# A Mamba and ternary FFN block on one core: x turned by DVE and DMA from the third block on, the first FFN up product in the second unit, fewer state steps at both ends

## The reference, cut to what matters

```
xn = layernorm(x)                                # x: 2 x 2048 tokens, 512 features
xz = xn @ in_proj_w.T;  x_branch, z = split(xz)  # 1024 features each
x_branch = silu(conv1d(x_branch, 4 taps) + conv_b)
X, dt, B, C = split(x_branch @ x_proj_w.T)
dt = softplus(dt @ dt_proj_w.T + dt_proj_b)
Y = ssd(X * dt, -exp(A_log) * dt, B, C) + X * D   # chunked scan with a carried state
attn = (Y * silu(z)) @ out_proj_w.T
hidden = sigmoid(xn @ q(w1).T) * (xn @ q(w2).T)   # 1408 wide
out = x + attn + hidden @ q(w3).T
q(w) = clip(round(w / (mean(abs(w)) + 1e-8)), -1, 1)
```

## Time and profile before

| what | value |
|---|---|
| median of 3 runs | 1642.5 us (1642.33 to 1643.32) |
| profiled execution | 1641.94 us, its span 1639.8 us |
| granted clock, whole span | 0.99 |
| PE, DVE, ACT, POOL busy | 1574.9, 1201.3, 890.4, 531.8 us |
| length of one block from block 1 on | 195.9 us |

### The profile page before, as it was taken

One profiled execution on the slowest core, in us unless ns is written; L12 is line 12 of the kernel. 1 busy time (PEld: TensorE's weight loads), 2 busy tenths in 40 slices (PEclk: granted clock), 3 DMA queues, 4 the chain that ended last, 5 costly groups with the idle time before them and its releaser, 6 DMA issues.

```text
span 1639.8 us, 25533 instructions
## 1 busy us (share of the span) xinstructions
PE 1574.9 (96%) x9206; PEld 757.0 (46%) x9206; DVE 1201.3 (73%) x1868; ACT 890.4 (54%) x1848; POOL 531.8 (32%) x502
## 2 busy tenths in 40 slices
PE   6788899999999999999999999999999999999999
PEld 3334444544444444444445444444444444444444
DVE  7877876698566985689746996569955698567972
ACT  6686526565356644466355663646535564456641
POOL 4246673243033421234121431314403243133320
PEclk9899899999999999999999999999999999999999
DMA  7154430142102330133201332023310233002420
GB/s 262 63 175 138 148 108 14 60 106 72 35 27 68 99 93 1 40 84 91 72 7 47 88 86 59 8 59 91 83 46 27 62 94 94 10 27 73 103 58 26
DMA packets 175613, 119.08 MB, mean 73 GB/s; under 512 B 125280, under 2 KB 127072, under 8 KB 175488
## 3 DMA queue, kind: packets, MB, share of 16 engines
q1 hardware_dynamic: 175488, 117.46, 25.3%
HBM read 94.09 MB, written 23.33 MB: 72 GB/s over the span
## 4 chain that ended last, share of the span: by engine, by line
PE 86%; issue 3%; DVE 2%; POOL 2%; ACT 2%; DMA 1%; DVEq 0%; POOLq 0%; SPq 0%; ACTq 0%
PE bank L564 18%; PE bank L674 17%; PE bank L692 9%; PE bank L474 9%; PE bank L647 9%; PE bank L458 9%; PE bank L484 4%; PE bank L596 3%; PE bank L608 2%; PE bank L581 2%; POOL less L1615 1%; PE bank L441 1%; ACT edc L923 1%; PE bank L631 1%; PE bank L496 0%
## 5 line engine op out<-in xcount | busy, mean ns | idle before, releaser
L564 PE MATMUL bank<-wx_hi,arena 128*128 128x512 f16 x1024 | 320.0, 383 | 0.0
L674 PE MATMUL bank<-xt_hi,q 128*128 128x512 f16 x704 | 267.8, 380 | 0.1
L674 PE MATMUL bank<-xt_lo,q 128*128 128x512 f16 x704 | 267.7, 380 | 0.0
L1583 POOL TENSOR_TENSOR xst<-xdt,dst 128x512 f32<-128x512 f32 x64 | 66.8, 1043 | 487.2 <-DVE xdt L1241 487.2
L564 PE MATMUL bank<-wx_lo,arena 128*128 128x512 f16 x512 | 196.1, 383 | 0.0
L692 PE MATMUL bank<-q,arena 128*128 128x512 fp8e4 x704 | 163.7, 381 | 0.0
L923 ACT ACTIVATE edc<-csl,csv 128x128 f32<-128x128 f32 x512 | 155.6, 387 | 0.8 <-DMA csl<-sums 0.8
L564 PEld LDWEIGHTS bank<-wx_hi,arena 128*128 128x128 f16 x1024 | 101.1, 99 | 115.1 <-issue 4.3
L1287 DVE TENSOR_TENSOR edc<-edc,gt 128x512 f32<-128x512 f32 x128 | 129.1, 1048 | 31.4 <-ACT edc L928 31.3
L1604 POOL TENSOR_TENSOR yac<-yac,xs 128x512 f32<-128x512 f32 x64 | 95.4, 1491 | 152.4 <-DVE yac L1308 152.4
L962 ACT CAST arena<-full 128x512 f16<-128x512 f32 x88 | 54.5, 619 | 148.0 <-DVE full L1354 148.0
(11 more groups left out here) (219 smaller groups left out, 3539.5 us busy)
## 6 DMA issues: line engine op xcount, KB each, us to landing
csl<-sums SPq DMA_DIRECT2D x128, 256.0 KB, 3.7
y_squares<-xs SPq DMA_DIRECT2D x56, 256.0 KB, 2.0
yac<-y_squares SPq DMA_DIRECT2D x168, 64.0 KB, 2.5
res<-x SPq DMA_DIRECT2D x32, 256.0 KB, 3.0
out<-res SPq DMA_DIRECT2D x32, 256.0 KB, 2.0
raw<-w_ffn SPq DMA_DIRECT2D x25, 256.0 KB, 2.9
full<-w_ffn SPq DMA_DIRECT2D x17, 256.0 KB, 4.2
yac<-x SPq DMA_DIRECT2D x16, 256.0 KB, 3.7
```

The source lines that it names most:

```text
L564: i = pe.matmul(banks[0][:], act[:, k, c * P:(c + 1) * P], wt[:, k, hf * half:(hf + 1) * half], start=(n == 1), stop=(n == 3 * ki))
L674: i = pe.matmul(up_bank(m, j)[:], q12[:, j, m, k, :], part[:, k, :], start=(n == 1), stop=(n == 2 * kd))
L1583: pool.tensor_tensor(by_head(xst[:], hd), by_head(xdt[:], hd), heads_over(sml["dst"][:, c, :], hf * hph, hph, hd), ALU.mult).then_inc(S["x ...
```

## The change

Six things.

1. From block 2 on x is not turned by PE. DVE transposes the normalised chunks in 32x32 squares (`squares_of_x`, four more transposes a block), SP writes them to DRAM and reads them back in four DMAs of 256 KB each, runs of 32 floats (`turn_x`, issued behind the up products). ACT and DVE make `xt_hi` and `xt_lo` from SBUF. `turn(b + 1)` stays for block 1 alone. The first `x_branch` product moves to (0, 8), the last to (1, 10) (`FOLLOWING_LATER`).
2. The next block's x is loaded ahead of `load_res(b, 3)`, and the statistics are done two chunks at a time beside up products 2 and 3, the root beside 4, the normalising and the squares beside 5 and 6.
3. In blocks 1 to 7 PE does `ffn_up(b, 0)` at the end of unit 1, ahead of `project_z(b, 3)`, and no longer at the end of unit 6. ACT and DVE take its result where they did.
4. In block 0, units 0 to 3 have no state (it is zero): no `off_mm`, no yoff, no `sd`, no `y_skip`, and the state is written, not added to. The six memsets of it go.
5. In block 7, units 4 to 7 don't make a state that nobody reads: no `xe`, no `xst`, no `st_mm`, no `state`, no `st_hi` and `st_lo`. In its `ffn_down` chunks 2 and 3 come one behind the other.
6. The weight preparation has another order: scales come one or more steps later behind their sums, the last cuts beside the FFN are 1 and 3 steps in place of 2 and 2, and the last ternary pieces of DVE come behind `turned(1)` and `hid_lo(0, 10)`.

```diff
+FEWER = {"off_mm": 4, "yoff": 4, "sd": 4, "y_skip": 4}
+BESIDE_FFN = [2, 2, 2, 2, 2, 2, 2, 1, 3]
+FOLLOWING_LATER = {(0, 8): 0, (0, 10): 1, (1, 0): 2, (1, 2): 3, (1, 4): 4, (1, 6): 5, (1, 8): 6, (1, 10): 7}
...
-    prep = list(kinds("O M O M O M O M  O M O M O M O M  M M M S M M M B  T M T M T M M M  T M T M T M T S "
-                      "M T M B T M M T  M T M T M M M M  M T S T B T " + "T T " * beside_ffn))
+    prep = list(kinds("O M O M O M O M  O M O M O M O M  M M M S M M M M  M B M T M T M T  M T M T M T S M "
+                      "M T M T B T M T  M T M T M M M M  S T T T T B " + "T " * sum(BESIDE_FFN)))
...
+        def x_squares(j):
+            return x_dram.rearrange("c (i a) (k j b) -> j a k (c i) b", a=SQ, b=SQ, j=P // SQ)[j]
...
+            def turn_x(b):
+                for c in range(chunks):
+                    sp.wait_ge(S["x_blocks"], at(b - 2, "x_blocks", c))
...
+                    sp.dma_start(x_dram[c], xsq[c]).then_inc(D["x_out"], DMA)
+                sp.wait_ge(D["x_out"], (b - 1) * chunks * DMA)
+                for j in range(P // SQ):
+                    sp.dma_start(xall[j * SQ:(j + 1) * SQ].rearrange("a k (n b) -> a k n b", b=SQ),
+                                 x_squares(j)).then_inc(D["x_sq_in"], DMA)
...
+                    if b and b < nb - 1 and m == 0:
+                        for c in range(chunks):
+                            load_x(b + 1, c)
+                    if b and b < nb - 1 and m == 7:
+                        turn_x(b + 1)
...
-                    update(b, u)
+                    if goes_on(b, u):
+                        update(b, u)
...
+                    if b and u == 1:
+
+                        ffn_up(b, 0)
                     if u + 2 < len(units):
                         project_z(b, u + 2)
-                    elif b and u == 6:
-                        ffn_up(b, 0)
...
-                if b < nb - 1:
+                if b == 0:
                     turn(b + 1)
...
+                for together in ((0,), (1,), (2, 3)) if b < nb - 1 else ((0,), (1,), (2,), (3,)):
...
+            def squares_of_x(b, c):
+                dve.wait_ge(S["xn"], at(b, "xn", c))
+
+                dve.wait_ge(S["diag_mm"], at(b - 1, "diag_mm", 12 + c))
+                dve.transpose(xsq[c], xin[c]).then_inc(S["x_blocks"], 1)
...
+                    elif b and b < nb - 1:
+                        if m in (2, 3):
+                            statistics(b + 1, 2 * m - 4)
+                            statistics(b + 1, 2 * m - 3)
+                        elif m == 4:
+                            root(b + 1)
+                        elif m in (5, 6):
+                            for c in (2 * m - 10, 2 * m - 9):
+                                normalise(b + 1, c)
+                                squares_of_x(b + 1, c)
+                if b < nb - 1:
+                    turned(b + 1)
+                hid_lo(b, kf - 1)
                 if b == 0:
                     for kind, n in last:
                         prep_second(kind, n)
-                if b < nb - 1:
-                    turned(b + 1)
-                hid_lo(b, kf - 1)
```

More of the change, by code:

```diff
@@ L122, in mamba_ffn_block @@
               *(f"early{n}" for n in range(6)),
-              *(f"beside{n}" for n in range(4)), "sums_out", "sums_in0", "sums_in1",
-             "y_out0", "y_out1", "y_in0", "y_in1")}
+              "beside0", "beside1", "sums_out", "sums_in0", "sums_in1",
+             "y_out0", "y_out1", "y_in0", "y_in1", "x_out", "x_sq_in")}
         def sb(name, shape, dt=F32):
@@ L188, in mamba_ffn_block @@
         xsp = [sb(f"xst_{p}", [P, half], F16) for p in ("hi", "lo")]
-        yac = [sb(f"yac{n}", [P, half]) for n in range(2)]
-        gate = [sb(f"gate{n}", [P, half]) for n in range(2)]
-        xin = [*yac, *gate]
+        xall = sb("xin", [P, chunks, dm])
+        xin = [xall[:, c] for c in range(chunks)]
+        yac, gate = xin[0:2], xin[2:4]
         edc = [sb(f"edc{n}", [P, hpg * P]) for n in range(2)]
@@ L267, in landing @@
                 s, landed = slot(4, n - n_early)
-                return ffn_ring[s], D[f"beside{s}"], landed
+                if s < 2:
+                    before = len(range(2 + s, len(loaded), 6))
+                    return ffn_ring[s], D[f"early{2 + s}"], before * DMA + landed
+                return ffn_ring[s], D[f"beside{s - 2}"], landed
             s, landed = slot(6, loaded.index((kind, n)))
@@ L446, in x_branch @@
                 bk = banks[4 + m % 4]
+                if b > 1 and m < 4:
+                    name, n = (("y_added", 7), ("yoff", 7), ("state", 7), ("attn", 3))[m]
+                    pe.wait_ge(S[name], at(b - 1, name, n))
                 if m == 0 and b:
@@ L790, in turned @@
                 for k in ks:
-                    act.wait_ge(S["x_turned"], at(b, "x_turned", k))
+                    if b < 2:
+                        act.wait_ge(S["x_turned"], at(b, "x_turned", k))
+                    elif k == 0:
+                        act.wait_ge(D["x_sq_in"], (b - 1) * (P // SQ) * DMA)
                     if b and k == 0:
                         act.wait_ge(S["up_mm"], at(b - 1, "up_mm", 21))
-                    act.copy(xt[0][:, k, :], banks[4 + k][:]).then_inc(S["xt_hi"], 1)
+                    act.copy(xt[0][:, k, :], banks[4 + k][:] if b < 2 else xin[k]).then_inc(S["xt_hi"], 1)
             def x_branch(b, m):
@@ L808, in x_branch @@
                                ACT.Copy, scale=1.0 / (XN_SCALE * W_SCALE)).then_inc(S["raw"], 1)
+                if b > 1 and m == 4:
+                    act.wait_ge(D["x_out"], (b - 1) * chunks * DMA)
                 if b:
@@ L883, in project_x @@
                     act.wait_ge(D[f"y_out{u % 2}"], rounds(b, u) * DMA)
+                elif u >= 2 and not has_state(b, u - 2):
+                    act.wait_ge(S["y_added"], at(b, "y_added", u - 2))
                 elif u >= 2:
@@ L1071, in scalar_program @@
                         project_z(b, u + 2)
[L1072 removed]
+                    if goes_on(b, u):
+                        split_state(b, u)
                 for m in range(kf):
@@ L1618, in gpsimd_program @@
             pool.memset(mhalf[:], -0.5).then_inc(S["cleared"], 1)
-            for b in range(batches):
-                pool.memset(state[b][:], 0.0).then_inc(S["cleared"], 1)
-                for part in state_parts[b]:
-                    pool.memset(part[:], 0.0).then_inc(S["cleared"], 1)
             pool.memset(hal[:], 0.0).then_inc(S["cleared"], 1)
```

135 lines of the change are left out of this document (87 added, 48 removed).

## The result

The changed kernel took **1617.15 us** (median of 4, 1615.01 to 1617.57), the kernel before, on the same chip, 1642.83 us. The ratio is 0.984, 95% interval 0.983 to 0.986: faster by 25.7 us. The forecast was 1620.7 us, 21.8 us faster, so it was short by 3.9 us of gain.

What follows compares the result with a forecast made beforehand. PE was taken as the bound (96% busy, seven of eight blocks packed at 195.9 us). Gains 9.8 + 1.2 + 2.6 + 2.0 + 6 + 0.2 = 21.8 us from 1641.94 gave 1620.1, with 0.6 for the median 1620.7; range 1610 to 1634.

Steps and rivals of the forecast that it cites:

- x turned by DVE and DMA: Turn of x for six blocks: sixteen PE transposes go, net 1.64 us a block, 9.8 us in all.
- The DMA term: Reads of x's squares: 7.8 us to issue four, 1.9 to land; taken as zero cost, at most 12 us.
- the slack of 0.7 us: End of the up products: x's squares land at 832.9, on time by 0.7 us for ACT's xt_hi.
- Rival A: x's squares land late, up to 2.0 us in each of six blocks: 1622 to 1633 us; chance 0.22.
- The first up product: Moved to unit 1: covers PE's scan waits, 1.97 us a block; DVE's residual sum leaves 0.2, 1.2 us in blocks 1 to 6.
- Block 7: Last block: 2.6 us from 12 state matmuls gone, and 2.0 us from the moved up product kept whole.
- the 0.2 at the end: End of the last block: DVE starts on chunk 3, alone last, 0.2 us earlier.
- Block 0: Missing state products and reordered weight preparation: 12.8 us touched, half taken as gain, 6 us; bounds -2 to 12.8.
- B: DVE doesn't hold PE at attn(2), the 1.97 us stays whole, 10.6 us more: 1610 us; chance 0.08.
- C: Turn's gain lost behind it, as dt waits for DVE's s_lo and out_ready(2); 9.8 not gained: 1630 us; chance 0.09.
- D: Slower: x's reads don't overlap, 40 us, ending 30 late: 1800 us; decides from 3.7 us late; chance 0.06.
- E: No change: block 0 gives nothing, C holds, the DVE bound costs 4 us: about 1641 us; chance 0.05.

Runs made afterwards that it cites:

- e1: Changed kernel with the first up product of blocks 1 to 7 back at the end of unit 6: 1622.27 us, ratio 0.988.
- e3: Changed kernel with x turned by PE again in all blocks and loaded as before: 1630.09 us, ratio 0.992.
- e2: Changed kernel with DVE's second residual sum of blocks 1 to 7 moved ahead of y's low half: 1615.89 us, ratio 0.983.
- e7: Changed kernel with normalisation and squares of x in blocks 1 to 6 one up product later on DVE: 1660.32 us (one run).
- e6: Changed kernel with block 7 making its state again for the second half of its units: 1621.37 us, ratio 0.987.
- e5: Changed kernel with block 0 carrying its zero state through the first four units again, memsets back: 1616.44 us, ratio 0.984.
- e4: Changed kernel with the whole old order of block 0's weight preparation: 1621.63 us, ratio 0.987.
- e10: Changed kernel with the second half of the old preparation order (cuts 2 everywhere, last ternary pieces ahead of turned(1)): 1618.54 us, ratio 0.985.
- e9: e2 with, in addition, all four normalisations and squares of x at up product 5 on DVE: 1611.17 us, ratio 0.981.

## Why the prediction was right, and where it was off

**x turned by DVE and DMA: right in size.** Forecast 1.64 us a block; e1 gives 1.67, the undisturbed blocks of e3 1.6 to 1.9. The DMA term was also near: the four reads landed 10.1 us after the first issue (619.18 to 629.28), forecast 7.8 + 1.9 = 9.7, though by another split (5.8 to issue, and more to land) and for another reason: the forecast let each issue cost 1.94 us by its 2048 runs, and the first of each four takes 0.57. That the sum came near is luck. The write took 2.04 us (617.14 to 619.18), as taken from the earlier trace rows. But the slack of 0.7 us wasn't there: the last square ended 11.9 us ahead of the last hidden product (617.14, 629.06) where 12.3 was forecast, and the landing took 0.4 more. The recorded sign for this, "ACT's xt_hi released by PE, not by a DMA", failed in four blocks of six; in the changed kernel:

```profile
629.28 2.18 ACT L851 CAST xt_hi<-xin 128x512 f16<-128x512 f32 x4 [1.42 <-DMA xin<-x_squares]
```

PE paid 0.5 us in all for it, because it was 0.9 us later anyway for the residual sum. Rival A was thus right on the mechanism and wrong on the price in this kernel; e2 shows the price once the other cap is gone, and e7 how steep it is behind that.

**The first up product: the term that was mis-sized.** Forecast 0.2 us a block, measured 0.7. The form was right: no wait at unit 2's scan, and a new one at `project_out` 6 that the residual sum ends, in blocks 1 to 6 and not in block 7. It is 0.91 us, not 1.7 (1.56 in block 1, behind a late read-back):

```profile
786.34 0.63 ACT L1015 ACTIVATE yt_hi<-xs 128x512 f16<-128x512 f32 x1 [4.86 <-DMA xs<-y_squares]
...
787.43 0.67 DVE L1421 SCALAR_TENSOR_TENSOR yt_lo<-xs,yt_hi 128x512 f16<-128x512 f32 x1
788.82 0.68 DVE L1433 SCALAR_TENSOR_TENSOR res<-bank,res 128x512 f32<-128x512 f32 x1
...
789.56 0.39 PE L696 MATMUL bank<-wo_hi,yt_hi 128*128 128x512 f16 x1 [0.91 <-DVE res L1433]
```

The failing step is the reading of 799.14 as the place of the sum in "DVE without a gap". In the kernel before, that block had a gap: DVE's low half of y waited for a late read-back of Y. The same places there, first in the block that was read, then in block 6:

```profile
797.27 0.63 ACT L953 ACTIVATE yt_hi<-xs 128x512 f16<-128x512 f32 x1 [6.00 <-DMA xs<-y_squares]
797.93 0.69 DVE L1331 SCALAR_TENSOR_TENSOR yt_lo<-xs,yt_hi 128x512 f16<-128x512 f32 x1 [0.61 <-ACT yt_hi L953]
799.14 0.68 DVE L1343 SCALAR_TENSOR_TENSOR res<-bank,res 128x512 f32<-128x512 f32 x1
...
1384.01 0.63 ACT L953 ACTIVATE yt_hi<-xs 128x512 f16<-128x512 f32 x1 [5.04 <-DMA xs<-y_squares]
1384.94 0.67 DVE L1331 SCALAR_TENSOR_TENSOR yt_lo<-xs,yt_hi 128x512 f16<-128x512 f32 x1
1386.32 0.68 DVE L1343 SCALAR_TENSOR_TENSOR res<-bank,res 128x512 f32<-128x512 f32 x1
```

Against the first x_branch of its block (641.54 and 1229.24) the sum stands at 157.60 and at 157.08. So 0.52 us of the 1.7 were a late DMA. It was no single bad block: in blocks 1 to 7 the sum stands at 157.74, 157.32, 157.60, 157.33, 158.17, 157.08 and 157.08, late in five of seven. What the forecast didn't see is that this lateness mostly goes in the changed kernel (one block of six, the one of 1.56 us), and nothing shows why it goes. DVE's lateness from the moved product was 0.46 and not 0.65 (the sum at 788.82 is 115.79 behind the block's first B product at 673.03; the undisturbed 157.08 is 115.33 behind it). 1.7 - 0.52 - 0.19 = 0.99, against 0.91 to 0.92 measured. In six blocks (0.7 - 0.2) x 6 = 3.0 us. In the two profiles the span fell by 24.6 us, 2.8 more than the forecast's 21.8, and the six blocks by 12.4, where the forecast's terms (9.8 + 1.2, less the 1.3 of the moved down matmuls) gave 9.7: the miss lies here. The medians' 3.9 differ from this by what the runs scatter.

**Block 7: right.** 2.6 + 2.0 were forecast. e1 gives 2.0 for the up product, e6 3.6 for the state, because with it the wait of 1.0 us comes back: the forecast had put that into the other term. The last stretch fell by 6.1 us; the forecast's share there was 6.1: 2.6, 2.0, the 0.2 at the end, and 1.3 for three pairs of down matmuls that now stand ahead of the first x_branch. No run tried the 0.2 by itself; from the start of the last matmul to the end of the span it is 3.9 us before (1635.91) and 3.6 after (1611.59).

**Block 0: the right number for half a reason.** 6 was forecast, taken as half of 12.8, and the two profiles differ by 6.03. But 2.6 of the 12.8 us were PE's products with the missing state, and e5 shows that part, with DVE's 2.4 that stood beside the sum, at 0.5, nothing that could be told; the order of the preparation is worth 5 to 6 by e4. Half of 12.8 was a choice and no working, so that it came out is luck. (The 1.4 for the later xt_lo in that sum stands in no line of the earlier trace rows; e10, which puts these pieces back, shows 1.5, all of it at the turn.) The recorded warning, that a wait taken from one place shows up in the next, fits both: the earlier trace rows had 5.2 us at the scales, now 1.0, and 4.0 us have come ahead of the first up product.

**The rivals.** B (no cap on DVE) is out: the wait is there, and it costs 0.9 us. C (the turn's gain lost behind it) is out by the 1.67. D (reads that don't overlap) is out: 10.1 us for 16 x 64 KB, not 40. E falls with C. D's point of decision, 3.7 us late, was set too far out: it counted only the lateness itself, and e7, with PE waiting 5.45 us a block, is 44 us above the changed kernel and 17 above the kernel before. In e7 the clock makes the wait cost 1.4 times its own length (7.6 for 5.45).

## What to carry to other kernels

Read the place of an instruction on a packed engine in several blocks before you work with it, and look at what waited ahead of it: the sum stood between 157.08 and 158.17 us in seven like blocks, for a DMA that was late in five of them, and 0.52 of that took the term down to 0.2 us where 0.7 was measured. When the bounding engine waits for one thing only, find what is second before you remove it; here the two stood within a microsecond of each other, and only taking both (e9) gave the gain. In a stage that hangs on loops between engines, work taken from the bounding engine can be worth nothing, as in e5 (2.6 us of products, 0.5 in time): look first for a wait of that stage that ends on it.

## What the runs showed of the hardware that was not expected

- TensorE's clock after a wait: at the 0.9 and 1.56 us waits of the changed kernel and the 1.81 us waits of the kernel before and e1 the granted clock stays at 1.00. After one and the same 2.1 us wait in block 0 it was 0.50 (1.2 GHz) in five profiles and 1.00 in five, and cost 1.7 us where it fell. After the 2.6 us wait of e3 it was 0.50 in the stretch from 1184 to 1186 us, and after the 6.55 us wait of e7 until about 849 us.
- Runs of 128 bytes from DRAM in a 256 KB read: 1.48 us to issue and 5.7 to land in the median, against 0.43 and 3.3 in runs of 2 KB, with 1 MB in four reads in either case. The first of the four issues in 0.57 us with 128-byte runs too.
- The same read-back of Y (four DMAs of 64 KB) lets ACT wait 4.7 to 7.15 us in blocks 1 to 6 of kernels that don't differ in it. In one block of the kernel before and in the last three of e3 it is the write of 256 KB ahead of it that is late (3.2 to 4.4 us to land, 2.0 in all other blocks of all profiles), else the reads. Nothing in the traces says why.
